# A graph layer on one core: before the third gather of a third, POOL waits for the third of a group in front

## The reference

```python
xn = _layernorm(x)                                   # 6250 x 256
m = xn[src] @ weights[:256] + edge_attr @ weights[256:]      # 106250 x 256
norm = where(deg > 0, rsqrt(max(deg, 1)), 0)         # deg: edges per destination
gnn = segment_sum(m * norm[dst], dst, 6250) + h_bias
# mix: q, k, v of xn; k and v normed by head; kv = k^T v / 6250; out = q kv;
#      gelu((out + xn) w1 + b1) w2 + b2 + xn
x = x + gnn + mix(xn)
# ffn: router on the mean row picks 2 of 8 experts for all rows;
#      layernorm(sum of weighted experts + input) of layernorm(x)
x = x + ffn(_layernorm(x))
```

## Time and profile before

| | |
|---|---|
| time, median of 3 runs | 1591.93 us (1590.64 to 1594.72) |
| the profiled execution | 1609.85 us, span 1608.1 us |
| PE busy, weight load busy | 1082.5 us (67%), 687.8 us (43%) |
| DVE, ACT, POOL busy | 685.6 us (43%), 530.8 us (33%), 919.3 us (57%) |
| gathers at L562 from `xn_table` | 807, mean 973 ns each |
| mean granted TensorE clock | 0.850 |
| DMA packets | 189376, 275.67 MB, mean 171 GB/s |

### The profile page before, as it was taken

One profiled execution on the slowest core, in us unless ns is written; L12 is line 12 of the kernel. 1 busy time (PEld: TensorE's weight loads), 2 busy tenths in 40 slices (PEclk: granted clock), 3 DMA queues, 4 the chain that ended last, 5 costly groups with the idle time before them and its releaser, 6 DMA issues.

```text
span 1608.1 us, 20064 instructions
## 1 busy us (share of the span) xinstructions
PE 1082.5 (67%) x6075; PEld 687.8 (43%) x6075; DVE 685.6 (43%) x1732; ACT 530.8 (33%) x1116; POOL 919.3 (57%) x974
## 2 busy tenths in 40 slices
PE   0155767666566666755776666666577759999997
PEld 0012323323223322323432333333343459999997
DVE  4733434334333344322233233242322446677675
ACT  3611111111111111111213333243233257767673
POOL 6166666676666666666666666666666103434342
PEclk9977888888877888877889778787888869999999
DMA  9975555565555555476777768777767230111111
GB/s 252 303 222 177 176 174 167 180 196 183 182 172 179 179 182 183 131 242 203 215 226 221 223 214 244 229 216 229 245 211 219 85 99 27 51 44 45 49 40 40
DMA packets 189376, 275.67 MB, mean 171 GB/s; under 512 B 19840, under 2 KB 160296, under 8 KB 188037
## 3 DMA queue, kind: packets, MB, share of 16 engines
q1 hardware_dynamic: 139424, 152.85, 31.7%
q0 software_dynamic: 39888, 108.97, 22.5%
q10 hardware_dynamic: 9975, 12.80, 2.3%
HBM read 248.95 MB, written 25.60 MB: 171 GB/s over the span
## 4 chain that ended last, share of the span: by engine, by line
PE 33%; another core or an unknown queue 23%; issue 18%; DVE 13%; ACT 6%; DVEq 5%; DMA 2%; SPq 1%; ACTq 0%; POOL 0%; POOLq 0%
PE bank L1190 8%; PE bank L1179 4%; PE ps_t L1179 4%; DVEq L1367 4%; PE bank L926 4%; PE bank L957 4%; PE bank L1009 3%; DVE acc L1372 2%; PE bank L1040 2%; DVE lnst L1403 1%; PE bank L1052 1%; PE ps_t L938 1%; DVE xc L1399 1%; DVE st L1227 1%
## 5 line engine op out<-in xcount | busy, mean ns | idle before, releaser
L562 POOL DMA_INDIRECT ring<-xn_table,src_sb x807 | 785.0, 973 | 441.0 <-issue 224.9
L926 PE MATMUL bank<-ring,s 128*32 128x512 f32 x1662 | 272.2, 667 | 79.6 <-DVE s L1332 38.7
L1009 PE MATMUL bank<-wstage,xt 128*125 128x512 f32 x200 | 124.2, 748 | 108.3 <-ACT xt L629 73.1
L1372 DVE TENSOR_TENSOR acc<-acc,ps_t 128x160 f32 x277 | 89.2, 322 | 203.1 <-issue 155.2
L629 ACT ACTIVATE xt<-bank 128x250 f32<-128x250 f32 (+1 forms) x75 | 33.5, 447 | 307.7 <-remote 262.4
L1040 PE MATMUL bank<-xt,p_sb 128*128 128x250 f32 x200 | 73.6, 533 | 85.6 <-ACT xt L629 44.3
L957 PE MATMUL bank<-wg,acc 128*125 128x256 f32 x400 | 123.7, 471 | 7.6 <-issue 7.6
L926 PEld LDWEIGHTS bank<-ring,s 128*32 128x32 f32 x1662 | 42.3, 115 | 197.4 <-issue 147.4
L1643 DVE TENSOR_TENSOR h_lo<-h,h_hi 128x512 fp32r<-128x512 f32 x100 | 95.8, 967 | 49.0 <-ACT h_hi L629 49.0
L618 POOL TENSOR_TENSOR rx<-vex,half 125x2 f32<-125x2 f32 x25 | 17.5, 701 | 171.8 <-DVE nmx L1664 171.8
L1190 PE MATMUL bank<-fw_hi,h_hi 128*125 128x256 f32 x400 | 111.7, 279 | 0.0
(11 more groups left out here) (224 smaller groups left out, 2147.5 us busy)
## 6 DMA issues: line engine op xcount, KB each, us to landing
ring<-edges SPq DMA_DIRECT2D x207, 512.0 KB
ring<-xn_table,src_sb POOLq DMA_INDIRECT x807
xnr<-xn_table SPq DMA_DIRECT2D x25, 250.0 KB
xch<-x SPq DMA_DIRECT2D x25, 250.0 KB
base_rows<-xch ACTq DMA_DIRECT2D x25, 250.0 KB
xt_cols<-xte ACTq DMA_DIRECT2D x25, 250.0 KB
xtl<-xt_cols SPq DMA_DIRECT2D x25, 250.0 KB, 4.9
out<-res SPq DMA_DIRECT2D x25, 250.0 KB
```

What stands on the lines that cost most here:

```text
L562: pool.indirect_dma_start(out=to, out_offset=None, in_=rows, in_offset=bass.IndirectOffsetOnAxis(ap=index, axis=0),).then_inc(done, 16)
L926: mm = pe.matmul(ps_seg[t % 2][j * W:(j + 1) * W, :], lhsT=s32[:, t % 3, j * TS + i, :], rhs=ring[:, u, j, :], start=i == 0, stop=i == TS ...
L1009: mm = pe.matmul(ps_kv[0:TN, :], lhsT=xt[:, n % 2, c, 0:TN], rhs=wstage[:, c, :], start=c == 0, stop=c == KC - 1)
L1372: v.tensor_tensor(acc[:, :, ds(b, W)], acc[:, :, ds(b, W)], planes[:, :, j * W:(j + 1) * W], ALU.add).then_inc(s_acc, 1)
```

## The change

Before the third gather (j == 2) of a third, POOL waits until all gathers of the third before it have landed. The 24 gathers of the head stay as they are. From the changed line on, line numbers grow by 2.

```diff
             for q in range(RAW, NQ):
                 t, i = divmod(q, TS)
                 wait_past(pool, s_seg, q - RS + 1)
                 for j in strips(t):
                     c = column(t, j, i)
+                    if j == 2:
+                        pool.wait_ge(s_gat[(q - 1) % RS], arrived(q - 1))
                     gather(ring[:, q % RS, j, 0:D], src_sb[:, c:c + 1], s_gat[q % RS])
```

## The result

The changed kernel takes 1671.32 us (median of 4 runs, 1666.61 to 1672.08) against 1593.33 us (median of 4, 1590.64 to 1595.78): 1.0476 times the time before, with a 95% interval of 1.0455 to 1.0498. It is 78 us slower by the medians, and 76 us by the ratio, where 22 us were forecast.

What follows compares the result with a forecast made beforehand. PE and what it waits for were taken as the bound. Part two's 85.75 x (4.98 + 1.3) = 538.5 us against 505 is 33.5 us late; less 11 us of lead leaves 22, so 1592 + 22 = 1614 us, range 1588 to 1652.

Steps and rivals of the forecast that it cites:

- What bounds the kernel before: POOL is held by a full ring and isn't the bound; PE and what PE waits for are.
- Part one: 100 to 650 us, gathers beside key and value work: waits of 0 to 0.2 us a third, hidden, costing 0.
- part two: 735 to 1240 us, gathers beside the mix tiles, 85.75 thirds: 33.5 us late before the lead pays, 22 us after.
- The wait of 1.3 us for a third: In part two, the added wait was taken as 1.3 us a third, within bounds of 0 and 2.5 us.
- The slot waits of 0.91 us for a third: POOL's waits for a free ring slot in part two, 77.8 us, beside 4.98 us for a third back to back.
- The stretch: The costly waits were summed over part two only, 735 to 1240 us, 85.75 thirds.
- The lead pays part of it: In part two gathered data are 3 to 4 thirds ahead of PE; 2 thirds, about 11 us, were counted as spendable.
- The clock: PE's granted clock is 0.82 in part two; the prediction had no term for it.
- A: Rival: landings stay fast enough, mean wait under about 1.0 us in part two, no change, 1592 us; chance 0.27.
- B: Rival: POOL becomes the bound fully, edge loads delay gathers, wait 1.8 us or more, +56, 1648 us; chance 0.21.
- C: Rival: fewer gathers in flight let other loads land sooner, PE waits less, -5 us, 1587 us; chance 0.08.
- The price that the Trainium skill gives: About 2.0 us fixed plus bytes by 436 GB/s for a gather's DMA; no wait would be long, sum 0.

Runs made afterwards that it cites:

- e3: Changed kernel with the same 201 waits at the same place, but for the third two in front (q - 2); 1594.52 us, 0.9989 of the kernel before.
- e5: Kernel before plus a pause of four tile fills on POOL before each third gather from third 107 on, no landing wait; 1600.05 us, 1.0045.
- e1: Kernel before with the added wait only before the third gathers of thirds 6 to 106; 1602.68 us, 1.0042.
- e11: Kernel before plus a pause of seven tile fills on POOL before each third gather from third 107 on, no landing wait; 1677.01 us, 1.0509.
- e2: Kernel before with the added wait only from third 107 on; 1662.11 us, 1.0432.
- e13: Kernel before with the added wait only before the third gathers of thirds 120 to 139; 1620.48 us, 1.0107.
- e6: Changed kernel, but SP loads only half of the edge features from third 107 on; 1651.89 us, 1.0365 of the kernel before.
- e7: Kernel before, without the added wait, with half edge loads from third 107 on; 1595.56 us, 1.0005.
- e10: Kernel before, without the added wait, with each 250 KB mix transfer split into 112 and 13 partitions; 1594.90 us, 0.9994.
- e9: Changed kernel, but each 250 KB mix transfer of 125 partitions is issued as 112 and 13; 1637.57 us, 1.0247 of the kernel before.

## Why the prediction was right and wrong

- **What bounds the kernel before:** right. POOL is held by slots, a wait that is met is free (e3), and a pause that takes up all slot waits and 0.14 us more for each third costs 7 us (e5).
- **Part one hides its waits, part two doesn't:** right in kind. e1 gives +7 us where I had put 0: the waits in part one, 25.3 - 26 x 0.3 = 17.5 us in the changed kernel, weren't all covered by slot waits, though these were larger.
- **The wait of 1.3 us for a third:** right in size, 122.7 us over 100 thirds being 1.23 us, and partly by luck. Two errors cancel. With the waits in, the gathers land sooner: the packets of a third are through 2.7 us after its last issue in the mean of thirds 107 to 206, where before it was 3.2 us. But POOL goes on later than I had allowed, 1.45 us in the mean after the last packet of a landing that held it, and not 0.3 + 0.3 us.
- **The slot waits of 0.91 us for a third, all counted as slack:** the step that failed, and the largest. The new wait took over (69.0 - 13.7) / 100 = 0.55 us for a third. Over my 85.75 thirds the difference is 30 us. It has three parts. A wait line holds the fixed 0.3 us too, so of the 77.8 us in the earlier trace rows 38 x 0.3 = 11.4 us were no slack; the third back to back is 4.98 + 0.13 = 5.11 us, and the slot waits were 66 us. Of the slot waits 16.1 - 8 x 0.3 = 13.7 us remained beside the new ones. And the profiled execution of before was a slow one, 0.77 us of slot waits for a third where e3 has 0.69.
- **The stretch:** part two ended where I had drawn a window, 85.75 thirds. The late landings begin with third 107 or before, so it is 100.
- **"The lead pays part of it ... about 11 us":** the second step that failed, for this kernel. In e5 and e11 the lead pays as much, in e2 7 us by the same rows (1 us by the medians), and in the changed kernel nothing. The reason that I gave, that PE reads in bursts, limits what it covers (e13). Why the changed kernel kept none of it stays open.
- **The clock:** I had no term. e11 shows that none is needed while POOL sets the pace; beside the slot waits that remain, up to 14 us, its part isn't separated.

The account that holds for POOL is: its delay = new waits over the gap, less the slot waits given up. That much is arithmetic on its own time. For thirds 107 to 206 it is 122.7 - (69.0 - 13.7) = 67.4 us, where e2 measured +69. With e1's 7 us it is 74 of 76. My 22 us come to this with the slot waits (30), the shorter wait (-6), 14 more thirds at 67.4 / 100 = 0.67 us (10), the lead (11) and part one (7): 74 us.

Of the rivals, A is out. B named the full bound and was nearest in kind, since POOL's loop is the chain in part two; its signs were there, slot waits of 13.2 us between 735 and 1300 us and a lead of one third at 1000 us. But its source, the edge burst, is the smaller part (e6), and its wait of 1.8 us wasn't reached. It put +56 by a wait too long, slot waits given up whole and a lead that pays 20 us. C had nothing to it: e7 and e10 take bytes away or spread them in the kernel before, and it stays the same.

The price that the Trainium skill gives, page "DMA: Bandwidth & Descriptors", section "Anatomy of one DMA — SWDGE (gpsimd) path", would have made no change. It agrees with the 2.5 us that the prediction reads in part one, and not with the stretch of the mix tiles, where 67 landings held POOL for 1.8 us each over the gap.

## What to carry to other kernels

A wait that is put on an engine with slack is paid from that slack third by third: add up the new waits, take away the old ones that vanish, expect some of the old ones to stay, and take the fixed issue gap out of all before comparing. A lead of data over its reader is no slack of that kind. It is spent once, however long the delay lasts, and where the reader works in bursts it covers no more than its smallest value; here between nothing and 14 us of a lead of 18 to 23. When a producer has to wait for its own transfers, wait for one that is old enough: here one more third back costs nothing, one gather earlier costs some 145 us more.

## What the runs showed of the hardware

I hadn't expected, when I made the prediction, that a transfer of 125 partitions lies on so few DMA engines, and that this makes others late. The queue of ACT's stores in the changed kernel, as in the kernel before:

```profile
q10 hardware_dynamic: 9975, 12.80, 2.3%
```

Of these 9975 packets, 25 x 250 are the 1 KB rows of `base_rows`, 25 x 128 the rows of `xt_cols`, and 525 are left: 25 x (16 + 5), if a store of 128 partitions ends with a packet on each of 16 engines and one of 125 on 5. The split of e9 adds 600, which is 25 x (16 + 13 - 5), so the count of 5 fits a second time. A gather of 128 rows has 48 packets; if they are spread evenly, 3 for each of 16 engines (the trace doesn't name the engine of a packet), it is whole only when the slowest of them is done. With the split the waits for it fell from 122.7 to 80.5 us.

The Trainium skill, page "DMA: Bandwidth & Descriptors", section "Why a DMA increments its semaphore by 16 and not by 1", says that the number of engines is the largest up to 16 that divides the slowest dimension on both sides, which for 125 is 5. The packet counts agree. That such a transfer holds up those of other queues is in the waits above; how the queues share an engine, no run here shows.
